# Linear attention with a leaf tree: waits of TensorE placed singly, the residual one unit later, late values added ahead of queries

## The reference, cut to what matters

```python
xn = layernorm(x)
# attention: 16 heads of 64, causal and linear, phi(z) = elu(z) + 1
Q, K, V = phi(xn @ Wq + bq), phi(xn @ Wk + bk), xn @ Wv + bv
# per head, over the tokens i:
KV += outer(K[i], V[i]); Ks += K[i]
out[i] = (Q[i] @ KV) / (Q[i] @ Ks + 1e-6)
attn = out @ Wo + bo
# tree: 255 sigmoid gates, 256 leaf probabilities (products of gates along a path)
gate = sigmoid((xn @ Wq_tree.T) @ routers.T)
tree = (leaf_probs(gate) @ leaf_values) @ Wout_w.T + Wout_b
return x + attn + tree
```

## Time and profile before

| | us |
|---|---|
| median of three runs | 1342.34 |
| profiled execution | 1346.16 |
| its span (first to last instruction) | 1344.4 |
| PE (TensorE) busy | 1266.5, 94% |
| DVE (VectorE) busy | 844.0, 63% |
| ACT (ScalarE) busy | 622.1, 46% |
| POOL (GpSimd) busy | 373.8, 28% |

### The profile page before, as it was taken

How to read it: one execution, slowest core, us unless ns; L and a number is a source line. 1 busy time by engine, 2 the same in 40 slices (tenths; PEclk the granted TensorE clock), 3 DMA queues, 4 the chain that set the end, 5 groups by cost and what they waited for, 6 DMA issues and landing times.

```text
span 1344.4 us, 49015 instructions
## 1 busy us (share of the span) xinstructions
PE 1266.5 (94%) x22173; PEld 1115.1 (83%) x22173; DVE 844.0 (63%) x2186; ACT 622.1 (46%) x1007; POOL 373.8 (28%) x590
## 2 busy tenths in 40 slices
PE   5899999999989999999999999999999999999987
PEld 4789788888978888888888888889788887887977
DVE  4775766657576574765757566574766757666463
ACT  3553544435445253553536445353553535545351
POOL 3424132141421413223141411413223141321410
PEclk9899999999999999999999999999999999999999
DMA  6000001000000000001000000100001000000000
GB/s 211 18 3 18 18 3 33 3 33 3 10 26 2 33 3 10 26 2 33 2 19 18 10 26 2 34 3 10 26 3 33 3 17 18 2 18 3 17 2 18
DMA packets 21599, 25.95 MB, mean 19 GB/s; under 512 B 1025, under 2 KB 19728, under 8 KB 21392
## 3 DMA queue, kind: packets, MB, share of 16 engines
q1 hardware_dynamic: 21392, 22.82, 5.2%
HBM read 14.43 MB, written 8.39 MB: 17 GB/s over the span
## 4 chain that ended last, share of the span: by engine, by line
PE 78%; DVE 11%; ACT 6%; issue 4%; DMA 1%; SPq 0%; DVEq 0%
PE w_pair L646 16%; PE s_pair L646 16%; PE o_pair L658 8%; PE s_pair L658 8%; PE kv_pair L727 5%; PE o_pair L752 5%; PE o_pair L766 5%; PE s_pair L716 4%; DVE xn L506 3%; PE w_pair L693 3%; PE w_pair L698 3%; ACT ex L407 3%; PE w_pair L680 3%; ACT ex L410 3%; DVE v_aug L529 2%
## 5 line engine op out<-in xcount | busy, mean ns | idle before, releaser
L329 POOL TENSOR_SCALAR_AFFINE_SELECT aT<-aT 64x512 f32<-64x512 f32 x256 | 167.6, 655 | 896.3 <-ACT aT L434 888.0
L646 PE MATMUL w_pair<-xnT,wk 128*128 128x512 f32 x768 | 209.5, 409 | 6.2 <-issue 3.6
L646 PE MATMUL s_pair<-xnT,wq 128*128 128x512 f32 x756 | 195.3, 394 | 0.2 <-issue 0.2
L434 ACT ACTIVATE aT<-s_pair 128x512 f32<-128x512 f32 x128 | 76.5, 597 | 251.6 <-PE s_pair L716 251.6
L577 DVE TENSOR_TENSOR snaps<-kv_pair,snaps 128x65 f32<-128x65 f32 x768 | 173.4, 226 | 26.4
L520 DVE SCALAR_TENSOR_TENSOR kT<-w_pair,bias_one,ex 128x512 f32<-128x512 f32 x128 | 95.9, 749 | 142.4 <-ACT ex L410 142.4
L646 PEld LDWEIGHTS s_pair<-xnT,wq 128*128 128x128 f32 x756 | 143.3, 190 | 32.0 <-issue 0.4
L646 PE MATMUL s_pair<-wv,xnT 128*128 128x512 f32 x648 | 168.6, 395 | 0.0
L646 PEld LDWEIGHTS w_pair<-xnT,wk 128*128 128x128 f32 x768 | 138.4, 192 | 33.1 <-issue 4.4
L410 ACT ACTIVATE ex<-ex 128x512 f32<-128x512 f32 x256 | 161.8, 632 | 8.1
L407 ACT ACTIVATE ex<-w_pair,neg_bias 128x512 f32<-128x512 f32 x130 | 89.4, 688 | 158.1 <-PE w_pair L646 158.1
(11 more groups left out here) (105 smaller groups left out, 2021.6 us busy)
## 6 DMA issues: line engine op xcount, KB each, us to landing
x_in<-in_L_attn_x_dram SPq DMA_DIRECT2D x16, 512.0 KB, 3.8
out_dram<-y_buf SPq DMA_DIRECT2D x32, 256.0 KB, 2.1
stage<-in_L_attn_Wv_dram SPq DMA_DIRECT2D x2, 512.0 KB, 8.1
stage<-in_L_attn_Wk_dram SPq DMA_DIRECT2D x2, 512.0 KB, 9.7
stage<-in_L_attn_Wq_dram SPq DMA_DIRECT2D x2, 512.0 KB, 10.8
stage<-in_L_attn_Wo_dram SPq DMA_DIRECT2D x2, 512.0 KB, 9.1
bv_all<-in_L_attn_bv_dram SPq DMA_DIRECT2D x1, 512.0 KB, 8.7
ffn_tok<-in_L_ffn_Wq_dram SPq DMA_DIRECT2D x1, 256.0 KB
```

The lines of the kernel that those rows point to most:

```text
L329: pool.affine_select(out=part, in_=part, compare_op=ALU.is_ge, fill=0.0, base=0, pattern=[[0, 2 * CH], [1, D]], channel_multiplier=-1).the ...
L646: last = pe.matmul(dst, l, r, start=i == 0, stop=i == len(steps) - 1)
```

## The change

- The residual of a block is computed by GpSimd in unit p = 1 in place of p = 0.
- In units p = 2 and p = 6 VectorE drains the value tile before the queries (`values_first`).
- TensorE's waits: the wait for `a_masked` of the next unit moves from the head of `from_chunk` to the second transpose of oT, one unit earlier; the waits for S0 and S1 ahead of the scores move to the first matmul that writes each of the two; the wait for `o_normed` ahead of oT is left out where the first fill of the unit is drained by VectorE, which does it after `norm` (its bank W1 is what oT waits for), and moves to the value fill in units p = 5 and 6.
- The `until(o_normed, n)` in `tiled` goes; unit n - 1 had already waited for that count.

```diff
-                if p == 0:
+                if p == 1:
                     residual(g)
                     pool.wait_ge(x_consumed, g + 1)
...
+            def values_first(fills, p):
+                if p not in (2, PAIRS - 2):
+                    return fills
+                return [f for f in fills if f[0] not in ("Q", "V0", "V1", "oT", "kT")] + \
+                    [f for f in fills if f[0] in ("V0", "V1")] + \
+                    [f for f in fills if f[0] in ("Q", "oT", "kT")]
...
-                for name, _ in unit_fills(g, p, BLOCKS):
+                fills = [name for name, _ in unit_fills(g, p, BLOCKS)]
+                for name in values_first(fills, p):
...
                 elif kind == "oT":
                     for c in range(CH):
+                        if c == 1 and g * PAIRS + i + 1 < UNITS:
+                            until(a_masked, 2 * (g * PAIRS + i) + 4)
...
-            def scores(n):
+            def scores(n, bank_free):
...
                     for h in range(2):
+                        if t == 0:
+                            bank_free(h)
...
+                def bank_free(h):
+                    if n:
+                        until(drained[(S0, S1)[h]], uses_before[n - 1][(S0, S1)[h]])
+                    else:
+                        until_drained(("gate", h, 0))
                 if n:
-                    for bank in (S1, S0):
-                        until(drained[bank], uses_before[n - 1][bank])
                     until(s_copied, n)
-                else:
-                    for i in range(2):
-                        until_drained(("gate", i, 0))
                 until_drained(("Q", p, g))
-                scores(n)
+                scores(n, bank_free)
...
-                    if n:
-                        until(o_normed, n)
...
-                for name, bank in unit_fills(n // PAIRS, n % PAIRS, BLOCKS):
+                fills = unit_fills(n // PAIRS, n % PAIRS, BLOCKS)
+                first_by_vector = fills[0][0][0] in ("V1", "xT", "leaf")
+                for name, bank in fills:
...
-                    if bank in (O0, O1) or kind == "oT":
+                    if kind == "V0" and n % PAIRS in (5, 6) or kind in ("oT", "y") and not first_by_vector:
                         until(o_normed, n + 1)
```

## The result

| us | before | after |
|---|---|---|
| median of four runs each | 1340.88 (1339.39 to 1344.98) | 1275.51 (1273.15 to 1279.89) |
| profiled execution | 1346.16 | 1273.15 |
| its span | 1344.4 | 1271.4 |

The ratio is 0.9507, 95% interval 0.9477 to 0.9538: 65 us faster. The prediction had 38 and a range of 1290 to 1322, so it was too small and the time lies outside the range.

The account below looks back on a forecast made before the run. TensorE was taken to bound the kernel, so only its pauses could yield time. Residual 16, values 12 and pauses 10 summed to 38 us, giving a median of 1304 us, range 1290 to 1322.

Parts of the forecast that it names:

- What bounds the kernel: TensorE works 94% of the span; time can go only where it pauses: before kT, before outer products, in unnamed pauses.
- Residual one unit later: In p = 0 GpSimd's residual delays VectorE's xn and so kT; moving it to p = 1 gains 16.2 us.
- Values ahead of queries: Draining values first ends the outer products' stall of 0.38 us at p = 3 and 7, 31 times: 12 us.
- New places of waits: The mask's wait at oT has 1.5 us to spare and single waits inside fills show no bubble: 0 us.
- The unnamed pauses ... I take 10: TensorE pauses at ends of 256-instruction packets, 37 us in all; the change gains 10, bounds -5 and 20.
- do hold up TensorE's sequencer: Rival: standalone waits, 220 of 438 in the small pieces, cost up to 16 us more: 1288 us, chance 0.05.
- the number of paying places: Packet ends in the units that cost a pause: 29 before, 33 after the change, priced at 0.6 us ordinarily.
- the values in p = 3: Pauses cost about 1.9 us in p = 3, where values had just held up TensorE, against 0.2 to 1.1 mostly.

Follow-up runs that it names:

- group back at oT: Kernel after with the wait for `o_normed` put back ahead of oT (108 separate waits): 1305.28 us, ratio 0.9754.
- given wait at oT: Kernel after with a second wait, for the long-given signal `kv_filled`, ahead of oT's first transpose, behind kT's wait: 1300.36 us, ratio 0.968.
- shifted kernel after: Kernel after with 32 more transposes (64 instructions) in the ramp, so all packet ends move by 64 instructions: 1277.7 us, ratio 0.9527.
- the values alone: Kernel before with only the values drained ahead of the queries in p = 2 and 6: 1326.54 us, ratio 0.9881.
- the kernel before with oT mended: Kernel before with one edit, the `o_normed` wait ahead of oT left out or moved to the value fill: 1300.26 us, ratio 0.9705.

## Why the prediction was wrong, step by step

**What bounds the kernel: right.** Time went only where TensorE paused, and the three entries of the earlier trace rows were the three sources. All three are gone.

**Residual one unit later: right.** 16 us predicted; 16.5 from start to start, 12.7 between medians (the interval of that ratio reaches from 9 to 16 us). Every xn is at 414 ns or below, the entry has its 3 cases, and nothing is held back in p = 1. The rule of the Trainium skill (SBUF — State Buffer, section "SBUF: two separate sides") agrees with both: drains that read PSUM ran beside the 2.42 us addition at their usual length, while xn, which reads SBUF alone, had been held for 2.2 us.

**Values ahead of queries: right.** 12 us predicted, 12.2 from start to start, 16.1 between medians (interval 9.5 to 22). The queries were not late.

**New places of waits: right.** Neither the mask's wait at oT nor the single waits inside fills show a bubble; after has no entry of the fills in its waits of PE.

| kernel | packet ends | begun under 0.9 us ahead: step | 0.9 to 2.3 us: step | over 2.3 us |
|---|---|---|---|---|
| before | 31 | 8: 1.8 to 2.2 us | 18: 0.3 to 1.1 us | 5 |
| group back at oT | 32 | 8: 1.6 to 2.0 | 13: 0.2 to 1.3 | 11 |
| given wait at oT | 32 | 4: 1.5 to 2.1 | 15: 0.2 to 1.3 | 13 |
| after | 31 | 0 | 0 | 31 (3.7 at least) |

In the last column the steps are the ordinary ones (0.04, and up to 0.34 where the next group begins). In the middle columns of these kernels the pause ends 2.2 to 2.8 us after the transfer began, with one exception of 3.4. In the kernel before, for example, the stretch from the transfer's begin to the pause's end runs from 236.30 to 238.77 (asked 0.35 us ahead, step 2.12), from 400.59 to 403.35 (0.63, 2.13), and at 951.2 (1.48, 1.12) and 741.1 (2.02, 0.44). So the price is about 2.5 us less the time by which the packet was asked for ahead. That is what stood as `issue` in the earlier trace rows, the short and the long ones alike. With an early request there is nothing to pay, wherever the ends fall; the end in `from_chunk` that cost 1.9 us in the shifted kernel after had its transfer begun only 0.78 us ahead. The tie to the separate wait shows in time as well: in the two kernels with a group at oT, the transfers behind the 26 and 22 pauses over 0.25 us all began 1.0 to 3.0 us after the last separate wait at oT had been passed.

**"The unnamed pauses ... I take 10": this step failed by the same mistake.** The mechanism (TensorE at the end of a packet of 256) was right. The Trainium skill (Advanced Engine Details and Errata, section "ISA Cache") has lines of 256 instructions, two of them. The 256 agrees. The same section of the Trainium skill gives TensorE 128 KB, more than two of its 16 KB lines; the traces side with two, since in no kernel did a packet's transfer begin more than about 295 instructions before TensorE reached the packet. So a request can run ahead of need only as far as the sequencer does. But I let the number of paying places carry the sum (33 against 29) and held the price for a property of the unit. In the kernel after the places in `from_chunk` are as many as before (31 and 31 in the table), and not one pays. The measured term is about 36 in place of 10. The two readings of the price, the values in p = 3 and luck of places, are refuted by the kernels with the values alone and with the shift of the kernel after; luck was worth 18 of the 38 us in the kernel before, but only while the requests came late.

**The rivals.** The one with the waits that "do hold up TensorE's sequencer" (1288 us, 0.05) named the agent. It had the wrong place (the small pieces, whose separate waits cost 6 us a group at most, not the lone one behind kT) and the wrong measure: I multiplied 328 waits by their own 0.05 us, and 108 of them brought 40 us, 0.37 each. The range ended at 1290 because the total of the pauses, 37 us, was never allowed to go. The upper bound of 20 for their gain rested on the count alone; the honest one was all of them, 27 more than the 10 taken, and 1304 - 27 = 1277 is next to the 1275.5 measured.

**Open.** Why the separate waits in the small pieces still cost 6 us a group in the kernel after, but hardly anything in the kernel before with oT mended, was not taken apart. What makes the sequencer ask for a packet is open too. That it asks when it leaves the one before is not enough: counted in the same way, past the ramp, in the kernel after every transfer began at most 1.8 us after TensorE had passed the end of the packet before, but in the kernel before 15 began 1.9 to 6.5 us after it (the one at 236.30 by 5.6 us). So it is shown that a separate wait behind kT's makes requests late, and what lateness costs, but not by which rule it makes them late, nor why in some units by 1 us and in others by 3.

## What to carry to other kernels

An engine's `issue` pauses that come at equal distances in its instructions are ends of packets; ask first how far ahead of the pause the sequencer was, not how many there are. A wait that needs an instruction of its own stands in line behind every wait queued before it, so keep such waits away from the places behind a wait that ends late: leave out the wait that another one implies, or put it where one wait stands alone. When a pause can't be priced by its cause, the bound of what an edit can gain is the whole of it.

## What the runs showed of the hardware

- A separate wait is free or dear by its place, not by its number: 126 of them ahead of the queries cost 3 us or nothing, some 110 behind kT's wait cost 25 to 30. The Trainium skill says only that such instructions appear where an instruction waits for several engines (Perfetto Trace Analysis, section "Identifying Dependency Chains"); every kernel here agrees, and the price is not there.
- Sixty-four more instructions in the ramp made the kernel before 18 us faster (0.986). While packets come late, a comparison of two kernels within 1.4% can be a comparison of their alignments.
- In the kernel after, no packet end in `from_chunk` had its transfer begun less than 3.7 us ahead, and about 2.5 would do: TensorE was fed without a pause through 256 instructions in 2.1 us of small pieces.
